# The last image pair finished image by image in two freed banks, and the engines' orders laid out anew, in a four-block image kernel

## The reference, cut to what matters

```
x = x + L0(_gn(x))   # row and column scans, mixed by a gate
x = x + L1(_gn(x))   # max over shifted neighbours, 1x1 product, gelu
x = x + L2(_gn(x))   # depthwise 11x11 convolution
x = x + L3(_gn(x))   # 1x1 in, 8x8 spectrum filter, 3x3 taps, gate, 1x1 out
```

```
x1, x2 = (t[:, :hid // 2], t[:, hid // 2:])
g = jax.nn.gelu(x1, approximate=False) * x2
return jnp.einsum('bchw,oc->bohw', g, w_out)
```

## Time and profile before

| what | value |
|---|---|
| time before, median of 3 runs | 201.09 us (200.58 to 202.3) |
| profiled execution, its own time | 200.13 us |
| its span, first to last instruction | 198.4 us |
| TensorE matmul busy | 168.1 us, 85% |
| VectorE (DVE) busy | 166.6 us, 84% |
| ScalarE (ACT) busy | 129.0 us, 65% |
| GpSimd (POOL) busy | 100.5 us, 51% |
| mean granted TensorE clock | 0.971 |

### The profile page before, as it was taken

How to read it: one execution, slowest core, us unless ns; L and a number is a source line. 1 busy time by engine, 2 the same in 40 slices (tenths; PEclk the granted TensorE clock), 3 DMA queues, 4 the chain that set the end, 5 groups by cost and what they waited for, 6 DMA issues and landing times. The chain is left out here.

```text
span 198.4 us, 3172 instructions
## 1 busy us (share of the span) xinstructions
PE 168.1 (85%) x814; PEld 114.3 (58%) x814; DVE 166.6 (84%) x431; ACT 129.0 (65%) x270; POOL 100.5 (51%) x184
## 2 busy tenths in 40 slices
PE   2898998689989999998987999499989897978272
PEld 1575645553444875795964558378658595855120
DVE  6668994869979689869979899998998979896992
ACT  3245679789999969488859959025657482826620
POOL 7527255723462271446475679153538659433440
PEclk9999999999999999999999999969999999999858
DMA  6992000110001010010000100001100010011002
GB/s 128 317 225 45 10 16 8 25 26 13 7 8 23 7 26 2 3 26 2 17 0 0 40 0 0 0 5 41 40 0 5 0 40 2 0 43 40 0 0 79
DMA packets 8273, 6.29 MB, mean 32 GB/s; under 512 B 6080, under 2 KB 6848, under 8 KB 8160
## 3 DMA queue, kind: packets, MB, share of 16 engines
q1 hardware_dynamic: 8256, 6.09, 12.3%
HBM read 2.94 MB, written 1.57 MB: 23 GB/s over the span
## 5 line engine op out<-in xcount | busy, mean ns | idle before, releaser
L474 PE MATMUL bank<-bumps,xw 128*96 128x208 f32 (+1 forms) x256 | 50.3, 351 | 0.0
L474 PEld LDWEIGHTS bank<-bumps,xw 128*96 128x96 f32 x256 | 41.6, 166 | 6.5 <-issue 2.0
L1099 POOL TENSOR_TENSOR upper<-upper 112x512 f32<-112x512 f32 x16 | 20.3, 1266 | 13.4 <-ACT upper L850 12.6
L1044 POOL TENSOR_TENSOR msq<-moments 96x2 f32<-96x2 f32 x24 | 7.5, 314 | 33.4 <-DVE moments L1245 33.4
L1453 DVE SCALAR_TENSOR_TENSOR bank<-below,weights,bank 112x512 f32<-112x512 f32 x24 | 18.0, 751 | 1.7 <-ACT below L842 1.1
L1231 DVE BATCH_NORM_STATS2 stats<-x 96x6 f32<-96x256 f32 x48 | 17.9, 412 | 0.3
L1048 POOL TENSOR_TENSOR rstd<-gvar,weights 96x2 f32<-96x2 f32 x24 | 16.7, 696 | 1.9
L1055 POOL TENSOR_TENSOR ln_rstd<-ln_var,weights 128x4 f32<-128x4 f32 x8 | 8.2, 1027 | 15.2 <-ACT squared L749 15.2
L502 PE MATMUL bank<-prod,weights 128*128 128x512 f32 x16 | 10.3, 732 | 6.1 <-DVE prod L1459 6.1
L850 ACT ACTIVATE upper<-centre,weights 112x480 f32<-112x480 f32 x24 | 14.9, 689 | 0.0
L801 ACT ACTIVATE v<-x,shift,rstd 96x256 f32<-96x256 f32 x16 | 8.6, 586 | 8.6 <-issue 8.6
(11 more groups left out here) (170 smaller groups left out, 425.1 us busy)
## 6 DMA issues: line engine op xcount, KB each, us to landing
out_channels<-x_out SPq DMA_DIRECT2D x8, 192.0 KB, 2.1
x_all<-x_channels SPq DMA_DIRECT2D x1, 768.0 KB, 11.4
weights<-weights_packed SPq DMA_DIRECT2D x1, 709.0 KB, 8.6
lines<-strip SPq DMA_DIRECT2D x4, 128.0 KB, 5.3
x_all<-x_channels SPq DMA_DIRECT2D x2, 192.0 KB, 3.8
x_all<-x_channels SPq DMA_DIRECT2D x1, 384.0 KB, 6.6
weights<-weights_packed SPq DMA_DIRECT2D x1, 338.0 KB, 5.6
seq<-gu_col SPq DMA_DIRECT2D x8, 32.0 KB, 2.0
```

The source lines that it names most:

```text
L474: last = mm(image[:, first:last_row, :], xw[j % 2][:, n, half, i, :], bumps[:, n, q + first:q + last_row, :], start=(n, half) == (0, 0), s ...
L1099: tt(a, a, b, ALU.add).then_inc(s["upper_sums_done"], 1)
```

## The change

The kernel is still in pairs, except that the last pair's `gate3`, `output_product3`, `add_block3` and `store` are done in two halves, one image each. The two output products go into banks 4 and 5 instead of bank 7. Besides, the order lists of TensorE, ScalarE, GpSimd and VectorE are written anew at many places, and some calls change engine: `copy_states` of pairs 1, 4 and 6 go from VectorE to ScalarE; `copy_v2_pixels` of pairs 0, 1 and 7 from ScalarE to VectorE; of the `weigh_pixels`, VectorE takes (0, 2), (2, 2), (3, 3) and (3, 7) from GpSimd and gives it (1, 2) and (1, 7); `add_h1_bias(4)` goes to VectorE and `add_h1_bias(7)` to GpSimd. One filler product before `to_spectrum(7)` goes, one comes before `mix_channels3(7)`, one before `output_product3(7)`, and one more stands early, in `spread_filter`'s old place.

```diff
             def output_product3(j):
                 pe.wait_ge(s["prod3_done"], j + 1)
-                mm(p_taps[j % 2][:, :], w("wout3"), prod3[j % 2][:, :], start=True, stop=True).then_inc(s["out_done"], 1)
+                if j == PAIRS - 1:
+                    pe.wait_ge(s["x3_done"], PAIRS)
+                    mm(p_last[0][:, 0:PIX], w("wout3"), prod3[j % 2][:, 0:PIX], start=True, stop=True
+                       ).then_inc(s["out_done"], 1)
...
+            def last_output_product3():
+                pe.wait_ge(s["prod3_done"], PAIRS + 1)
+
+                mm(p_last[1][:, 0:PIX], w("wout3"), prod3[(PAIRS - 1) % 2][:, PIX:N], start=True, stop=True
+                   ).then_inc(s["out_done"], 1)
```

```diff
+            def last_gate3():
+                m, at = (PAIRS - 1) % 2, slice(PIX, N)
+                tt(prod3[m][MID:CP, at], gelu3[m][MID:CP, at], p_taps[m][MID:CP, at], ALU.mult
+                   ).then_inc(s["prod3_done"], 1)
...
+            def last_add_block3():
+                m = (PAIRS - 1) % 3
+                dve.wait_ge(s["out_done"], PAIRS + 1)
+                tt(x_out[m][:, PIX:N], x3[m][:, PIX:N], p_last[1][0:C, 0:PIX], ALU.add).then_inc(s["x_out_done"], 1)
...
-            add_block3(6)
             gate3(7)
             add_block3(7)
+            last_gate3()
+            last_add_block3()
```

Of the new orders the diff shows a line or two (VectorE, then ScalarE):

```diff
             tap3(1, 2)
-            norm_squares(1, 6)
             tap3(2, 2)
...
             pad_filtered(7)
+            shift_filtered(7)
+            gelu_gate3(6)
             upper_taps(7)
-            gelu_gate3(6)
-            shift_filtered(7)
             gelu_gate3(7)
```

More of the change, by code:

```diff
@@ L566, in _ @@
             scan(3)
+            gate_product(2)
             block1_centre(0)
-            gate_product(2)
             change0(2)
@@ L573, in _ @@
             project(4)
+            change0(3)
             layer_norm_products(4)
-            change0(3)
             norm_means(2, 0)
@@ L628, in _ @@
             block1_maxima(4)
+            change0(7)
+            output_product3(0)
             transpose_v2(3)
-            output_product3(0)
             gate_product(6)
             mix_channels3(2)
-            transpose_h1(7)
             to_spectrum(2)
@@ L636, in _ @@
             from_spectrum(2)
+            block1_maxima(5)
             norm_means(2, 4)
-            gate_product(7)
-            block1_maxima(5)
-            change0(7)
             convolve(0, 3)
+            transpose_h1(7)
             transpose_v2(4)
             convolve(1, 3)
+            gate_product(7)
             norm_means(2, 5)
@@ L876, in _ @@
             normalise0(3)
-            gelu_h1(1)
+            copy_states(1)
             tanh_gate0(0)
@@ L972, in _ @@
             normalise1(6)
+            normalise3(3)
             copy_v2_pixels(5)
[L974 removed]
             copy_t_pixels(3)
@@ L1156, in _ @@
             sum_upper(0, 1)
+            add_h1_bias(7)
+            sum_upper(1, 1)
             weigh_pixels(0, 3)
-            weigh_pixels(3, 3)
-            sum_upper(1, 1)
             add_block0(6)
@@ L1618, in _ @@
             add_block1(0)
+            norm_statistics(2, 0)
             copy_h1(3)
-            norm_statistics(2, 0)
-            keep_filter()
+            norm_squares(2, 0)
             add_block0(2)
             gated_inputs(4)
-            norm_squares(2, 0)
             max_vertical_pairs(1)
-            norm_moments(2, 0)
             max_horizontal(1)
             max_vertical(1)
+            norm_moments(2, 0)
             max_neighbours(1)
             norm_statistics(1, 2)
+            layer_norm_h1(4)
             norm_squares(1, 2)
-            layer_norm_h1(4)
-            copy_states(4)
+            gated_inputs(5)
             norm_moments(1, 2)
@@ L1726, in _ @@
             norm_statistics(2, 4)
-            weigh_pixels(1, 3)
             tap3(2, 1)
+            tap3(3, 1)
             filter_spectrum(2)
-            tap3(3, 1)
+            weigh_pixels(2, 3)
+            weigh_pixels(3, 3)
             norm_squares(2, 4)
             gate0(6)
-            weigh_pixels(2, 3)
+            weigh_pixels(1, 3)
             tap3(4, 1)
@@ L1805, in _ @@
             tap3(1, 4)
+            copy_v2_pixels(7)
+            weigh_pixels(3, 7)
             tap3(2, 4)
             tap3(3, 4)
+            tap3(4, 4)
+            filter_spectrum(5)
             add_block2(6)
-            weigh_pixels(1, 7)
-            filter_spectrum(5)
-            tap3(4, 4)
+            tap3(5, 4)
             norm_statistics(3, 6)
-            tap3(5, 4)
             norm_squares(3, 6)
+            gate3(4)
             tap3(0, 5)
-            gate3(4)
             norm_moments(3, 6)
             tap3(1, 5)
+            add_block3(4)
             tap3(2, 5)
-            add_block3(4)
             tap3(3, 5)
```

255 lines of the change are left out of this document (137 added, 118 removed).

## The result

The changed kernel takes 202.61 us (median of 20 runs, 200.75 to 204.05), the kernel before 200.22 us (median of 20, 198.56 to 203.14). The ratio is 1.0127, with a 95% interval of 1.0097 to 1.0158: 1.3% or 2.5 us slower. It was forecast at 199.9 us. (Ratios here leave disturbed runs out and medians do not, so a ratio need not be the quotient of the medians beside it.)

What follows compares the result with a forecast made beforehand. TensorE was the bound from 58 to 101.7 us; from 102 us TensorE and VectorE alternate. Terms -3.1 + 0.9 + 1.0 gave -1.2 us: profiled 198.9, median 199.9 us, range 197.7 to 202.5.

Steps and rivals of the forecast that it cites:

- Step 1: Until 110 us: earlier filter and normalisation close TensorE's gaps of 0.91 and 0.59 us; gain 0.7 us.
- Step 2: 118 to 134 us: `norm_squares(1, 6)` no longer blocked by GpSimd, no long TensorE idling, no clock fall; gain 3.0 us.
- Step 3: Until pair 3's filter, about 141 us: VectorE has more work ahead of that filter; loss 0.9 us.
- Step 4: 146 us: `norm_squares(3, 4)` ahead of GpSimd's addition, but `norm_squares(2, 6)` waits some 0.6 us; gain 0.3 us.
- Step 5: 162 us: `weigh_pixels(3, 7)` waits 1.4 us for GpSimd, `filter_spectrum(5)` comes later; loss 0.9 us.
- rival B: Blocking at 121 us returns in the new place, TensorE idles, clock falls: +2.8 us, 203.9 us; chance 0.14.
- Step 6: The end: later last tap, bare gelu, halves in one chain, smaller last store, one filler; loss 1.0 us.
- The filler before `mix_channels3(7)`: Near the end on TensorE: a product of 1.13 us in a shorter gap; loss 0.2 us.
- rival C: The end: the split overlaps nothing but the first half's store; already in the sum, no chance of its own.
- Rival A: Blocking is short or the places don't meet, step 5 is 0: -2.1 us, 199.0 us; chance 0.38.

Runs made afterwards that it cites:

- the changed orders with the PSUM source and the whole end: Changed kernel with `weigh_pixels(3, 7)` reading its pixels from PSUM and the last pair's gate, product, addition and store whole again: 197.72 us, ratio 0.9848.
- the split alone: Kernel before with only the last pair's gate, product, addition and store done image by image in two banks: 200.69 us, ratio 1.0012.
- the moved call: Kernel before with only `norm_squares(1, 6)` moved behind `norm_squares(2, 5)` and `weigh_pixels(1, 4)` on VectorE: 198.21 us, ratio 0.9858.
- the three edits: Kernel before with `norm_squares(1, 6)` behind `weigh_pixels(1, 4)`, `norm_squares(3, 4)` ahead of `add_block1(6)`, and `weigh_pixels(1, 7)` reading from PSUM: 197.08 us, ratio 0.9823.
- second let-pass run: Changed kernel with GpSimd waiting for VectorE's `weigh_pixels(3, 7)` ahead of its second queued weighing, `weigh_pixels(1, 7)`: 199.43 us, ratio 0.9918.
- weighing-behind-the-filter run: Changed kernel with VectorE's `weigh_pixels(3, 7)` moved behind `filter_spectrum(5)`: 198.98 us, ratio 0.9863.
- the PSUM source alone: Changed kernel with VectorE's `weigh_pixels(3, 7)` reading its pixels from PSUM instead of their SBUF copy: 198.81 us, ratio 0.9883.
- the fillers: Changed kernel with two filler products on TensorE ahead of `from_spectrum(5)`, the late filter left as it is: 200.2 us, ratio 0.997.
- the first of the last two kernels: Changed kernel with the last pair whole, `weigh_pixels(3, 6)` and `weigh_pixels(3, 7)` from PSUM, and `add_block3(6)` behind the last tap again: 198.28 us, ratio 0.9865.
- the last kernel: Changed kernel, last pair whole, `weigh_pixels(3, 6)` and `(3, 7)` from PSUM, old places of `add_block3(6)`, `gate3(6)` and ScalarE's end order: 197.11 us, ratio 0.9874.

## Why the prediction was wrong

It forecast 199.9 us, no measurable change. The measurement is 202.61 us, 1.3% slower. Of the six steps five came out within 0.5 us of their numbers; one was too small by 3.9 us. The measured sizes of steps 1 to 4 come from the profile of the changed orders with the PSUM source and the whole end, which has no fall of the clock at 113 us. Profiles of kernels whose calls are the same up to 120 us (the split alone, the moved call, the three edits) are 0.6 us ahead of the one of before to 0.8 us behind it at 118 us, so sums from the start of the span are good to about 1 us, differences between two near places to much less.

- **Step 1** (forecast -0.7): -0.2 at `mix_channels3(1)`. The gap of 0.91 us before `from_spectrum(0)` shrank to 0.40 and that of 0.59 us went, but before them this profile is up to 1.4 us behind the one of before (at `mix_channels3(0)`, 89.0 against 87.6): 0.6 us since 18 us, the rest in small places, a wait of 1.18 us at `project(5)` at 55 us among them. The prediction had named such losses as what a walk misses. But -0.2 and -0.7 can't be told apart here.
- **Step 2** (forecast -3.0): -3.5 at `norm_moments(3, 3)`. The mechanism and the size were right, and moving one call alone shows it.
- **Step 3** (forecast +0.9): +0.5.
- **Step 4** (forecast -0.3): -0.3, but otherwise made up: -0.9 by 155 us, then +0.6 for `weigh_pixels(3, 6)`, a meeting with GpSimd at 153 us that the walk did not see.
- **Steps 1 to 4** came to -3.4 us at `tap3(0, 4)`, forecast -3.1. Run by itself this body is 3.0 us faster (ratio 0.9848).
- **Step 5** (forecast +0.9) **is the step that failed.** It measured +4.8 us in the profile: from -2.0 at `tap3(0, 4)` to +2.8 at `filter_spectrum(6)`. The meeting was foretold well: both instructions had come 2.0 us forward with the body, and with that added the addition starts at 162.0 us (forecast 161.95) and VectorE's weighing at 163.0 (forecast 162.9). Two things were mis-sized. The wait was taken as the rest of the addition and one queued weighing, 1.4 us, because two places in the rows of before had lasted two instructions. (A third, at 146.18, had lasted one, with nothing ready behind it on GpSimd.) Here the addition and all three weighings went ahead, so VectorE's weighing was held 3.0 us, 1.6 more than forecast. And the clock was put at nothing. With 3.18 us of idling it fell, for 2.2 us more: 0.9 + 1.6 + 2.2 = 4.7 us. The prediction had priced such a fall at 121 us, in step 2 and rival B (1.2 us), and did not ask for it here.
- **Step 6** (forecast +1.0): +1.1 in the profile, as the sum of +1.3 in the chain and -0.2 for the store; the split itself is 0.5 of it, by the profile of the run on the kernel before. The other half was given to pair 6's addition moving ahead of two taps. That was the wrong cause, so this number was right in part by luck: with the addition moved back the stretch got longer, not shorter (9.05 us against 8.58), because `upper_taps(7)` behind `gelu_gate3(6)` on ScalarE makes the last tap late, and the early addition only fills VectorE's wait.
- The filler before `mix_channels3(7)` (forecast +0.2) shows no cost, and the split did not overlap, as rival C had it.
- **Rival A** had step 5 at 0, for a wait of one instruction; it gives 199.0 and was the wrong way. **Rival B** ended on the right side, for the wrong place: nothing blocked at 121 us. Its mechanism, blocking, idling, fall of the clock, is what happened 40 us later.

The sum with the measured terms is -3.4 + 4.8 + 1.1 = +2.5 us, and by the ratio it is 2.5. That they agree to a tenth is chance: the ratio is good to 0.6 us and the profiles to about 1.

The Trainium skill, page "SBUF — State Buffer", section "Who interferes with whom", says that a VectorE instruction with two SBUF inputs contends with a GpSimd instruction that reads SBUF, that one with at most one SBUF input does not, outside VectorE's 2-port modes, and that the first to issue keeps the shared ports for its whole instruction. The runs agree with the first two (3.55 us against 0.56 for the same work with one operand in PSUM). The third they show only in part: VectorE's weighing waited for three weighings that GpSimd issued after it had come, so who waits does not always get in at the next instruction's end. The measurement decides here.

## What to carry to other kernels

When a VectorE instruction with two SBUF operands can meet GpSimd, price the wait at up to GpSimd's whole back-to-back queue from that moment, not at one or two instructions (here one queued weighing passed ahead in one place and three in another, and what decides is open), and then ask which engine idles behind it and whether TensorE's clock falls. Cures that cost nothing here: read one operand from PSUM where it lies anyway, put the instruction behind the one that others wait for, or give GpSimd a wait so that VectorE passes. A held instruction is worth curing only if what stands behind it is not waiting for something else until the same moment: of the three taken out of the kernel before, one gave 2.8 us by the ratio, one 0.7 by the profile and one nothing.

## What the hardware showed that I had not expected

- VectorE held through one, two and four back-to-back GpSimd instructions: 0.69, 1.65 and 3.55 us for a weighing of 0.56. GpSimd is hardly held in turn: its next addition took 1.58 us instead of 1.27 when VectorE's weighing at last ran, and in the kernel before its second weighing 1.31 instead of 0.99. Both started without a gap, so VectorE was let in without one.
- The granted clock fell within 3.18 us of idling in the changed kernel (1.00 from 164.2 to 165.0 us, 0.52 from 165.0 to 165.6) and behind 1.28 us in the second let-pass run, and did not behind 1.47 us after two fillers. It also fell in the weighing-behind-the-filter run where nothing but idle times of 0.63 and 0.65 us stood before, and at 113 to 118 us in the profiles of the changed kernel and of one other (0.66 in both), while eight kernels with the same calls there kept it full. Three of these ten (the PSUM source alone, the fillers, and the first of the last two kernels) also had one at 56 us (0.56 to 0.57 from 55.8 to 59.7), and the last kernel had one at 173 us (0.50). Such falls cost 1.0 to 1.7 us where they could be counted, at 113 and at 173 us. What decides between two executions of the same calls stays open; it may be part of the spread of 3 to 5 us that the kernel before and the changed one have in their times.
